# Gated delta recurrence on one core: the second batch row half a chunk behind the first, the state kept in PSUM

## The reference

```python
q = silu(conv(x @ Wq.T)); k = silu(conv(x @ Wk.T)) * DK**-0.5; v = silu(conv(x @ Wv.T))   # causal, 4 taps
a = sigmoid(x @ Wa.T + ba)          # decay per head and value channel
beta = sigmoid(x @ Wb.T + bb)       # rate per head
def step(S, ins):                   # S: (b, H, DK, DV)
    read = einsum('bhk,bhkv->bhv', k_t, S)
    err = read - v_t
    S = a_t * S - b_t * k_t * err
    o_t = einsum('bhk,bhkv->bhv', q_t, S)
# then: norm of o over DV, * ln_w + ln_b, * sigmoid(x @ Wg.T), @ Wo.T, added to x, layer norm
```

## Time and profile before

| what | value |
|---|---|
| runs | 2590.77, 2597.03, 2597.59 us; median 2597.03 |
| profiled execution | 2591.12 us, its span 2589.3 us |
| mean granted TensorE clock | 0.942 |
| busy in the whole span | PE 2260.6 us (87%), PE weight load 1728.4, DVE 1531.3 (59%), ACT 1060.7 (41%), POOL 457.1 (18%) |
| recurrence | from about 71 us to 1303 us |

### The profile page before, as it was taken

One profiled execution on the slowest core, in us unless ns is written; L12 is line 12 of the kernel. 1 busy time (PEld: TensorE's weight loads), 2 busy tenths in 40 slices (PEclk: granted clock), 3 DMA queues, 4 the chain that ended last, 5 costly groups with the idle time before them and its releaser, 6 DMA issues. The chain is left out here.

```text
span 2589.3 us, 44842 instructions
## 1 busy us (share of the span) xinstructions
PE 2260.6 (87%) x16524; PEld 1728.4 (67%) x16524; DVE 1531.3 (59%) x3305; ACT 1060.7 (41%) x2983; POOL 457.1 (18%) x868
## 2 busy tenths in 40 slices
PE   4888888888888888888849799999999999969997
PEld 3777777777777777777746556555556656666675
DVE  7566777667777666767747645545545545533334
ACT  2555445555444554544522344344344434412121
POOL 6321233322133332233310000000000000000000
PEclk9999999999999999999959899989989989989998
...
DMA packets 76174, 54.81 MB, mean 21 GB/s; under 512 B 6201, under 2 KB 72897, under 8 KB 74945
## 3 DMA queue, kind: packets, MB, share of 16 engines
...
HBM read 50.45 MB, written 1.57 MB: 20 GB/s over the span
## 5 line engine op out<-in xcount | busy, mean ns | idle before, releaser
L1410 DVE TENSOR_REDUCE b_nmax<-ps 128x1 f32<-128x1024 f32 (+7 forms) x256 | 194.1, 758 | 325.0 <-PE ps L1310 324.2
L1306 PE MATMUL ps<-b_kT,b_qT 64*128 64x512 f32 (+3 forms) x768 | 327.8, 535 | 17.3 <-issue 15.4
L1377 ACT ACTIVATE b_prob<-ps,b_nmax 128x1024 f32<-128x1024 f32 (+7 forms) x256 | 189.7, 741 | 342.3 <-DVE b_nmax L1410 342.2
L785 DVE TENSOR_TENSOR prod<-ps,mt 128x128 f32<-128x128 f32 x512 | 148.4, 290 | 294.2 <-PE ps L662 242.7
L328 PE MATMUL ps<-xT,taps 128*128 128x128 f32 x2176 | 299.0, 280 | 0.6 <-ACT vd L379 0.6
L501 POOL TENSOR_TENSOR di<-di 128x128 f32<-128x128 f32 x240 | 130.4, 543 | 786.1 <-DVE di L430 768.5
L328 PEld LDWEIGHTS ps<-xT,taps 128*128 128x128 f32 x2176 | 265.1, 191 | 4.3 <-ACT vd L379 0.9
L653 PE MATMUL ps<-ident,w 128*128 128x128 f32 x512 | 159.7, 312 | 108.1 <-DVE w L788 106.6
L746 ACT COPY wt<-ps 32x128 f32<-32x128 f32 x512 | 129.3, 255 | 242.9 <-PE ps L653 235.4
L1306 PEld LDWEIGHTS ps<-b_kT,b_qT 64*128 64x128 f32 x768 | 127.2, 191 | 120.0 <-issue 103.2
L1039 PE MATMUL ps<-xTn,f_w 128*128 x352 | 167.4, 611 | 24.9 <-PEq L948 18.5
...
## 6 DMA issues: line engine op xcount, KB each, us to landing
decay<-ends_dram SPq DMA_DIRECT2D x256, 128.0 KB, 5.0
...
```

The source lines that it names most:

```text
L1306: mm = pe.matmul(bank[:, 0:c1 - c0], lhsT=qT[rows, f, b * T + i * P:b * T + (i + 1) * P], rhs=kT[rows, f, b * T + c0:b * T + c1], start=Tr ...
L1377: nc.scalar.activation(prob[:, u % 2, 0:n], src, ACT.Exp, bias=nmax[:, u % 4:u % 4 + 1], accum_out=total[:, w % 4, h:h + 1]).then_inc(sems ...
L1410: nc.vector.tensor_reduce(nmax[:, u % 4:u % 4 + 1], src, axis=AX.X, op=ALU.max, negate=True).then_inc(sems["max_done"], 1)
```

## The change

1. **Order.** The loop runs over half chunks j = 0 to 7 of a section. Half j starts row x = j % 2 of chunk cc and does its blocks 0 and 1, while the other row y does its blocks 2 and 3, finish, outputs and update. Row 1 is thus half a chunk behind row 0 everywhere.
2. **State in PSUM.** Each row has a bank (4 and 5) that holds its state. PE adds the increment onto it (start=False), DVE multiplies bank and decay into `state`, and ACT `put_back` copies `state` into the bank again. The addition L799 is gone. Before the loop PE writes the zero state into the banks.
3. **Key masks on POOL.** The products are ring items p0 to p7 in banks 6 and 7, one in each half. ACT copies the transposed keys once into `kt`; POOL `pool_keys` makes the four masked copies in one 128x512 product.
4. **Pieces.** Each op of DVE's preparation becomes two, one for heads 0 to 3 and one for heads 4 to 7, spread over 32 quarter slots (`dve_piece`); the diagonal copy of `mt` goes to ACT (`act_diagonal`), the scaling of V to POOL (`pool_values`). `tmp` gets a buffer of its own. Item order is new.

The diff, cut to its core:

```diff
-        BOTH = [[["a0"], ["g0"]], [["a1"], ["a2"]], [["a3"], ["g1"]], [["b0"], ["b1", "b2", "b3"]],
-                [["c0"], ["c1"]], [["k0.0"], ["k0.1"]], [["k1.0"], ["k1.1", "var"]], [["q0.0"], ["q0.1"]],
-                [["q1.0"], ["q1.1", "rs0"]], [["rs1"], ["n0", "n1"]], [["n2"], ["n3", "v0.0"]], [["v0.1"], ["v1.0"]],
-                [["v1.1"], ["dt", "v2.0"]], [["v2.1"], ["v3.0"]], [["v3.1"], ["wo.0"]], [["wo.1"], ["yt"]]]
+        BOTH = [["k0.0"], ["k0.1"], ["k1.0"], ["k1.1", "p0"], ["a0"], ["c0"], ["a1"], ["c1", "p1"],
+                ["a2", "var.0"], ["var.1", "b0"], ["b1", "a3"], ["b2", "b3", "p2"], ["n0", "n1"], ["g0", "n2"], ["g1", "n3"],
+                ["p3"], ["rs0", "q0.0"], ["q0.1", "rs1"], ["q1.0"], ["q1.1", "p4"], ["v0.0"], ["v0.1"], ["v1.0"],
+                ["v1.1", "p5"], ["v2.0"], ["v2.1"], ["dt", "v3.0"], ["v3.1", "p6"], ["wo.0"], ["wo.1"], [], ["p7", "yt"]]
...
+        def product_of(f, j):
+
+            return NC * f + (j + 1) // 2, 1 - j % 2
 
...
+            elif kind == "p":
+                cc, b = product_of(f, int(j))
+                if cc % NC == 0 and cc:
+                    pe.wait_ge(S["copied"], 16 * (cc // NC))
+                keys = kq[:, cc // NC % 2, b, cc % NC, :, :, :, :, :].rearrange("p q i g h s -> p (q i g h s)")
+                pe.matmul(out[:, 0:2 * P], lhsT=keys[:, 0:P], rhs=keys, start=True, stop=True, skip_group_check=True)
+                mm = pe.transpose(out[:, 2 * P:3 * P], keys[:, 0:P], cst["ident"][:, :])
...
                 last_one = nc.scalar.copy(yT[:, :], out[:, 0:N])
+            elif kind == "p":
+                cc, b = product_of(f, int(j))
+                n = B * cc + b
+                act.wait_ge(S["g_kept"], n)
+                if n >= 3:
+                    act.wait_ge(S["k_kept"], n - 2)
+                last_one = nc.scalar.copy(kt[:, n % 2, :], out[:, 2 * P:3 * P])
...
+        def dve_piece(dve, ch, ring, f, nx, q, at_last):
...
+            if 8 <= q < 12 or 13 <= q < 16:
+                decays_piece(dve, ch, ring, f, nx, q - 8 if q < 12 else q - 13, 0 if q < 12 else 1)
+            if q in (12, 19):
+                rates_piece(dve, ch, ring, f, q // 19)
+            if 20 <= q < 25:
+                inverse_piece(dve, ch, ring, f, nx, q - 20, 0)
+            if 25 <= q < 30:
+                inverse_piece(dve, ch, ring, f, nx, q - 25, 1)
...
+        def inverse_piece(dve, ch, ring, f, nx, step, half):
+
+            blocks = slice(half * HB * NBLK // 2, (half + 1) * HB * NBLK // 2)
+            R = rr[:, :, :, :].rearrange("p h b (n i) -> p (h b n) i", i=BK)[:, blocks]
+            NN = gn[:, :, :, :, :].rearrange("p h b n e -> p (h b n) e")[:, blocks]
+            M = mt[:, nx, blocks, :, :].rearrange("p n i j -> p n (i j)")
+            t0, t1 = tmp[:, blocks, 0, :], tmp[:, blocks, 1, :]
+            if step == 0:
+                wait_kept(dve, ring, f, "n3" if half else "n1")
+                dve.wait_ge(S["r_made"], 2 * f + half + 1)
+                ch.step(tt(NN[:, :, 3:5], NN[:, :, 3:5], R[:, :, 2:4], ALU.mult))
+            if step == 1:
+                ch.step(stt(out=M[:, :, 4:16:5], in0=NN[:, :, 0:3], scalar=-1.0, in1=R[:, :, 0:3], op0=ALU.mult, op1=ALU.mult))
...
+        def act_diagonal(act, f, nx, half):
+
+            blocks = slice(half * HB * NBLK // 2, (half + 1) * HB * NBLK // 2)
+            act.wait_ge(S["r_made"], 2 * f + half + 1)
+            R = rr[:, :, :, :].rearrange("p h b (n i) -> p (h b n) i", i=BK)[:, blocks]
+            M = mt[:, nx, blocks, :, :].rearrange("p n i j -> p n (i j)")
+            nc.scalar.copy(M[:, :, 0:16:5], R).then_inc(S["diag_made"], 1)
+
+        def pool_values(pool, ring, f, nx):
+
+            wait_kept(pool, ring, f, "v3")
+            pool.wait_ge(S["d_done"], f + 1)
+            inv = di[:, 1, :, :]
+            vv = vd[:, nx, :, :, :].rearrange("p h b (c t) -> p (h b c) t", t=CH)
+            nc.gpsimd.tensor_tensor(vv[:, :, 1:CH], vv[:, :, 1:CH], inv[:, :, 0:CH - 1], ALU.mult).then_inc(S["prepared"], 1)
 
...
+        def pool_keys(pool, cc, b):
+            n = B * cc + b
+            if cc >= 2:
+                pool.wait_ge(p_ready[b], cc - 1)
+            nc.gpsimd.tensor_tensor(kfull[:, n % 4, :, :], kt[:, n % 2, :].unsqueeze(1).to_broadcast([P, G, P]),
+                                    cst["pair_rows"][:, :].unsqueeze(2).to_broadcast([P, G, P]), ALU.mult).then_inc(
+                S["k_kept"], 1)
+
+        def dve_masks(n, products):
+            nc.vector.tensor_tensor(gq[:, n % 4, :, :], products[:, 0:2 * P].rearrange("p (q r) -> p q r", q=2),
+                                    cst["head_masks"][:, :, :], ALU.mult).then_inc(S["g_kept"], 1)
 
...
                 def finish(cc, b):
                     n = B * cc + b
                     pe.wait_ge(wt_kept[b], NB * (cc + 1))
                     pe.matmul(ps[:, b, P:2 * P], lhsT=wt[:, b, :], rhs=gq[:, n % 4, 1, :], start=False, stop=True,
                               skip_group_check=True).then_inc(o_ready[b], 1)
+                    if n >= 1:
+                        pe.wait_ge(S["k_kept"], n)
                     if cc >= 1:
-                        pe.wait_ge(S["k_kept"], 4 * (nth(cc, b) + 1))
-                    for bb in range(B):
-                        if finished[bb]:
-                            pe.wait_ge(p_used[bb], finished[bb])
+                        pe.wait_ge(s_back[b], cc)
                     for g in range(G):
-                        mm = pe.matmul(ps[:, 4, g * P:(g + 1) * P], lhsT=kfull[:, n % 4, g, :], rhs=wt[:, b, :],
-                                       start=True, stop=True, skip_group_check=True)
+                        mm = pe.matmul(ps[:, 4 + b, g * P:(g + 1) * P], lhsT=kfull[:, n % 4, g, :], rhs=wt[:, b, :],
+                                       start=False, stop=True, skip_group_check=True)
                     mm.then_inc(p_ready[b], 1)
-                    finished[b] = cc + 1
-
-
...
+
+                for cc, x, f, j in halves:
+                    def ring(k):
+                        for item in both.slots[4 * j + k]:
                             pe_item(pe, both, f, 1 - f % 2, item, f + 1, f - 1)
...
-                    turn(cc, 1, 3)
-                    finish(cc, 0)
-                    ring(3, 1)
-                    finish(cc, 1)
+                    y, cy = 1 - x, cc - 1 + x
+                    start(cc, x)
+                    if cy >= 0:
+                        turn(cy, y, 2)
+                    ring(0)
+                    if cy >= 0:
+                        take_off(cy, y, 2)
+                    turn(cc, x, 0)
+                    ring(1)
+                    take_off(cc, x, 0)
+                    if cy >= 0:
+                        turn(cy, y, 3)
+                    ring(2)
+                    turn(cc, x, 1)
+                    if cy >= 0:
+                        finish(cy, y)
+                    take_off(cc, x, 1)
+                    ring(3)
+                turn(last_chunk, 1, 2)
+                take_off(last_chunk, 1, 2)
+                turn(last_chunk, 1, 3)
+                finish(last_chunk, 1)
 
...
-                    pool_prepare(pool, both, f, 1 - f % 2, 1)
-                    pool_gate(pool, ch, both, f)
+                for cc, x, f, j in halves:
+                    nx = 1 - f % 2
+                    if j or f:
+                        of, oj = (f, j - 1) if j else (f - 1, 2 * NC - 1)
+                        wait_kept(pool, both, of, f"p{oj}")
+                        pool_keys(pool, *product_of(of, oj))
+                    if j == 1:
+                        pool_prepare(pool, both, f, nx, "near")
+                    if j == 3:
+                        pool_rstd(pool, ch, both, f)
+                        scan(ch, nc.gpsimd.tensor_tensor, f, nx)
+                    if j == 5:
+                        pool_gate(pool, ch, both, f)
+                    if j == 6:
+                        pool_prepare(pool, both, f, nx, 0)
+                        pool_prepare(pool, both, f, nx, 1)
+                    if j == 7:
+                        pool_values(pool, both, f, nx)
 
...
+                def put_back(cc, b):
+                    act.wait_ge(s_ready[b], cc + 1)
+                    nc.scalar.copy(ps[:, 4 + b, :].rearrange("p (g v) -> p g v", g=G), state[:, b, :, :]).then_inc(s_back[b], 1)
+
...
+                    if cy >= 0:
+                        keep(cy, y, 2)
+                    ring(0)
+                    keep(cc, x, 0)
+                    if cc >= 1:
+                        put_back(cc - 1, x)
+                    ring(1)
+                    if j in (4, 6):
+                        act_diagonal(act, f, 1 - f % 2, j // 6)
+                    if cy >= 0:
+                        keep(cy, y, 3)
+                    ring(2)
+                    keep(cc, x, 1)
+                    ring(3)
+                keep(last_chunk, 1, 2)
+                keep(last_chunk, 1, 3)
 
...
```

(42 more changed lines are left out.)

287 lines of the change are left out of this document (91 added, 196 removed).

## The result

The changed kernel takes 2630.68 us (median of 4 runs, 2627.86 to 2643.22), the kernel before on the same chip 2597.31 (4 runs). The ratio is **1.0143, 95% interval 1.0106 to 1.0181**: slower by 1.4%, where 2572 was forecast. The profiled execution spans 2625.8 us against 2589.3, 36.5 more.

What follows compares the result with a forecast made beforehand. It took four engines passing one small tile around, none full, as the bound. A section of 72.2 + 0.8 + 2.0 = 75.0 us saves 16 x 1.8 = 29, +4 outside, total -25: 2572 us, range 2500 to 2640.

Steps and rivals of the forecast that it cites:

- What bounds the kernel: Recurrence: four engines pass one small tile around, none full; 76.8 us a section, so what counts is where queues meet.
- The walk: Eight half chunks of a section followed on PE's and DVE's queues: sum 72.2 us, plus 0.8 for small waits.
- POOL beside DVE: Seven POOL ops a section stand where DVE prepares: bounds nothing to 7 x 1.0 plus 0.5 us, taken as 2.0.
- DVE's relief: Eight state additions (0.69 each), diagonal copy and V scaling leave DVE: some 58 to 53 us a section.
- W 2.88 and 1.08: PE's waits in H1 and H4 for ACT's kept turns, behind table loads, activations and copies: 2.88 and 1.08 us.
- Clock: Slow clock in the recurrence costed at nothing afterwards, near 1.00; if it stays, up to 3 us a section more.
- no change: Rival: slow clock stays with each section, 76.6 us a section, total +1, 2598 us; chance 0.10.
- Outside the sections: Last half alone +5, short first -2, prologue +3.5, tail -2.5 us: +4, between -2 and +10.
- POOL holds DVE: Rival: each of seven meetings costs the whole 1.0, V twice: 80.5 us a section, 2660 us; chance 0.27.
- clean interleave: Rival: POOL and DVE miss each other, ACT's late work hides: section 71.5 to 73 us, 2527 us; chance 0.23.
- DVE's halved inverse ops above their price: Sign: beside POOL's L569 and L510, by over 1 us in four places or more, means the slower case.
- A row's updates: Sign in the recurrence: state updates of one row would stand 18.7 us apart.

Runs made afterwards that it cites:

- g1: Changed kernel with the gate's two products moved from POOL to DVE, and ACT's diagonal copies and table loads moved to other places: 2554.06 us, 0.9866 of the kernel before.
- experiment 4: Also e4: changed kernel with POOL's key masks, V scaling and gate all shrunk to one column or element, waits kept: 2534.85 us, 0.9788 of the kernel before.
- experiment 9: Changed kernel with the gate's products on DVE and the state not kept in PSUM, DVE adding the old state again: 2655.09 us, 1.0248 of the kernel before.

## Why the prediction was wrong

**What bounds the kernel** was right: four engines around one tile, no engine full, the price of a section decided by what DVE does ahead of a solve, and by what ACT does ahead of a kept turn (g1).

**The walk** was right in its sum, 72.2 + 0.8 against the 73.1 of experiment 4. By halves, measured in the changed kernel from one first solve's reduce to the next (section from 709.44 us): H0 7.50, H1 9.69, H2 9.76, H3 9.34, H4 11.17, H5 11.41, H6 10.97, H7 8.05; the walk had 7.83, 9.93, 8.97, 9.39, 10.89, 8.82, 9.36, 7.03. H0, H1, H3 and H4 are within 0.4, and the whole miss but for 0.8 in H2 is in H5 to H7 (+2.6, +1.6, +1.0), where POOL's long ops stand.

**The step that failed** is "POOL beside DVE ... I take 2.0: two meetings paid in full ... and the others missed or absorbed". It measured **5.6 to 5.8** (78.66 - 73.10 by the sections; 92 us / 16 by the times), inside my bounds of 0 to 7.5 but near the upper one. 4.2 of it is direct, the rest the slow clock that follows. In the terms of my sum a section is 72.4 without POOL and slow clock, 4.2 for POOL and some 2.0 for the clock, where I had 72.2 + 0.8, 2.0 and nothing. Two reasonings carried the 2.0, and both were wrong. I took L439's 1.0 in the earlier trace rows as the price of a meeting; it is the remainder of whatever POOL op has started, 1.9 for the V scaling. And I read the two long medians as "both pay here"; in each meeting only the second pays, and L516's 0.64 had been paid to another DVE op, the copy L438. The argument that a key product and piece 3 start together, so that at most the second op is hit, was no protection: in H5 the second op is hit (L487, 1.16 instead of 0.39). The Trainium skill's rule ("SBUF — State Buffer", Who interferes with whom), of which I wrote that the trace agreed in kind, puts up to a whole POOL op on a meeting; the traces bear that out, and I should have laid POOL's queue over DVE's pieces as I did for PE.

**DVE's relief** was right in direction: the additions are worth 66 us by experiment 9, and with POOL's products shrunk the change brings the 2.1% of e4, which leaves work out.

**ACT.** The diagonal copy takes 1.14, not 0.6, and H4 is a little longer than the walk (11.17 against 10.89); the state's copy back into PSUM is 0.58 against my 0.59. I priced the waits that ACT's late copies cause (W 2.88 and 1.08) and did not ask what it would bring to move them: 33 us.

**Clock.** I costed it at nothing and wrote near 1.00; it is 0.97, from 0.96. That term failed too: each section keeps 4.9 us at 0.50, which is some 2.0 us of its length by the table (78.7 - 76.6), within the "up to 3" that I had set aside. The walk's sum holds without it. The "no change" rival did not happen.

**Outside the sections**: +6.7 (36.5 - 29.8) where I had +4. First update +4.5 (94.0 against 89.5; I had +3.5), the last half alone and the short first +7.4 (1248.7 - 1211.5 - 29.8; +3), tail -5.2 (2625.8 - 1342.7 against 2589.3 - 1301.0; -2.5).

**The rivals.** "POOL holds DVE" is what happened, at 78.66 instead of its 80.5 a section and 2631 instead of 2660. I gave it 0.27; it decides from 3.5 us a section, and 5.6 came. With the bounds at 0 and 7.5 and no row for the overlap, 3.5 was nearly the middle, and a chance near one half would have been the honest reading. The "clean interleave" rival (71.5 to 73) is nearly experiment 4 (73.1). Of the signs that I named, "DVE's halved inverse ops above their price ... by over 1 us in four places" came out as 1.9, 1.0, 0.9 and 0.8, two of them beside L559, which I had not named: by its letter the sign said no to a rival that came. A row's updates are 19.7 us apart, not 18.7, and H5 is the longest half, not H4.
